# Expert attention units: the scores for the row maxima computed for two heads at once, in the two 64-row halves of TensorE's array

## The chip, the cores and the metric

The kernel runs on one core of one Trainium2 chip. The metric is device time in microseconds; the kernel before took 4004.94 us (median of 3 runs, 4000.94 to 4005.34). TensorE is PE in the profile, its weight loads PEld, VectorE DVE, ScalarE ACT, GpSimd POOL, and SyncE, which issues most DMAs, SP.

## What is computed

A two-layer model on x of 4 x 1024 tokens x 256 channels, all float32, each block behind a layer norm and added to x:

1. causal attention, 16 heads of 16, with a per-head linear position bias;
2. a mixture of four attention experts: a router picks the top 2 of 4 experts for each token, and each expert runs full (not causal) attention over the tokens of one batch that chose it:

```
q, k, v = xg @ wq[e] + bq[e], xg @ wk[e] + bk[e], xg @ wv[e] + bv[e]
att = softmax(where(valid_key, einsum(q, k) * 0.5, -1e9))
out += weight * (att @ v @ wo[e] + bo[e])      # scattered back to the tokens
```

3. causal attention with rotary positions;
4. a mixture of 64 small gated networks, top 8, capacity 128, beside a shared one.

## The kernel before, in words

The change touches block 2. Its 16 expert units (4 batches x 4 experts) run one after the other, sorted by size. A unit has `nt` tiles of 128 gathered tokens. There are three kinds of program: the first unit, the 14 middle ones, and the final one, each written out for every `nt` from 1 to 8; a run jumps from unit to unit through a barrier of all engines. In this run the 14 middle units have 7 tiles (4 units), 6 tiles (3), 3 tiles (4) and 2 tiles (3); the first unit has 6 tiles and the final one 2.

Within a unit, heads go in four groups `g` of four heads. Each group goes through two passes.

- **Pass 1** (task `s1`, L817 on PE) computes the scores with queries on partitions, only for the row maxima. q and k are float32 values split into three bfloat16 parts (hi, mid, lo) that lie under each other on the partitions of QS and KS, so that a matmul over 96 rows adds six part products; row 96 is the mask of the valid keys, and so a score matmul has 99 rows. A task fills one of two PSUM slots of two banks: one head with all its keys if there are over 512, two heads if over 256, four otherwise. One DVE reduction (L1086) per task takes the maxima into M. After a group's last one, `mh` and `ml` (L1094, L1099) split the negated maxima in two bfloat16 parts, `mt` (L827) transposes them, ACT copies them to MR, and a DMA that POOL issues (`mr`, L620) writes them into rows 99 and 100 of QS.
- **Pass 2** goes in key tiles `kt` and chunks of up to 512 queries `qc`; such a pair is called a round here. In a round, four `s2` matmuls (L835, 101 rows, one per head) write scores minus maximum into three single PSUM banks in turn, ACT takes the exponentials (L1023), and one `pv` task (L857, eight float32 matmul instructions of 17 columns, four heads in four column strips of the array) adds the products with the values. The result goes through `po` (ACT), `nt` (a PE transpose into one of pass 1's two slots, then DVE), and at the unit's end `yt` and `op` (L879, L1155).

Pass 1 of groups 1 to 3 runs in the unit itself, beside pass 2 of the groups before; pass 1 of group 0 of the *next* unit runs at the end, beside pass 2 of group 3. For that the next unit's rows are transposed (`xt`), projected (`qp`, L748), split on POOL (`spl`), stored to DRAM (`qs`, L1594, SP) and loaded back as the stacked rows of QS and KS (`ql`, L1610, SP, three DMAs for each of q and k and each group); `mk` (L1671) loads the mask rows. `nv` and `nr` on SP fetch the next weights and rows.

Each engine takes its tasks in one common order. That order is written by `unit_order`: every task gets a due time in a time scale of its own (`step` for one group of pass 2, `pace` for one group of pass 1, `turn` for the way from pass 1 to pass 2), and the list is sorted by it. PE, DVE, ACT and SP each work strictly down their part of the list, so a task that waits holds up all behind it on its engine.

## Time and profile before

| | |
|---|---|
| median of 3 runs | 4004.94 us |
| the profiled execution | 3994.29 us, its span 3992.6 us |
| mean granted TensorE clock | 0.932 of full speed |
| to about 840 us | block 1 |
| from there to 1018.6 us | the first unit |
| 1018.6 us to 2663.5 us | the 14 middle units |
| 2663.5 us to 2727.6 us | the final unit |
| from there to the end | blocks 3 and 4 |

The trace is one execution. A row of a timeline gives start, duration, engine, line, operation, output and inputs, the number of instructions that were merged into it, and in brackets how long the engine was idle before it and on whom it waited. A row of the windows gives the stretch, its length, the busy time of PE, PEld, DVE, ACT and POOL with their instructions, the granted clock, the DMA share and GB/s. The duration of a matmul holds the length of the pipeline, so what one costs in a stream is read from the distance of starts, not from its duration. The boundaries of the units are the ends of the last L1155 of each.

### The profile page before, as it was taken

The numbers are of one execution on the slowest core, as the hardware profiler recorded it, in microseconds if no ns is written. First come the engines' busy times: TensorE is split into PE (matmuls) and PEld (weight loads), VectorE is DVE, ScalarE is ACT, GpSimd is POOL, SyncE is SP. The second block draws the span as 40 slices with busy tenths as digits, with TensorE's granted clock in tenths as the row PEclk, the third lists the DMA queues.
The fourth block names the chain that finished last, engine by engine and source line by source line (L and its number), as shares of the span: only waits on it lengthen the run. The fifth ranks groups of instructions, "written<-read, shape, count | busy, mean of one in ns | idle before, by whom it ended". The sixth has DMA issues, their size and how long they took to land.

```text
span 3992.6 us, 56810 instructions
## 1 busy us (share of the span) xinstructions
PE 3415.7 (86%) x21573; PEld 1652.4 (41%) x21574; DVE 2375.3 (59%) x3496; ACT 2091.3 (52%) x4546; POOL 988.4 (25%) x845
## 2 busy tenths in 40 slices
PE   6999999878899999998899888764799888888895
PEld 3444445333434333334334334332344344445674
DVE  5565655656575757575675554333767878785323
ACT  2666665545576666665665554331465455551221
POOL 1241522322202020202111123232434141200574
PEclk8999999979999999999999999776899999998897
DMA  6454536323313030303313134334333232203588
GB/s 187 151 163 124 156 102 203 83 81 88 88 28 95 22 95 22 95 22 88 77 42 84 46 102 115 101 106 103 97 91 114 77 108 58 85 27 121 138 196 227
DMA packets 307098, 399.90 MB, mean 100 GB/s; under 512 B 33677, under 2 KB 271931, under 8 KB 299893
## 3 DMA queue, kind: packets, MB, share of 16 engines
q1 hardware_dynamic: 275718, 341.63, 30.9%
q0 software_dynamic: 26880, 50.49, 5.4%
q10 hardware_dynamic: 4224, 4.19, 0.3%
q8 instruction: 162, 2.65, 0.3%
q14 instruction: 114, 0.93, 0.1%
HBM read 230.48 MB, written 156.17 MB: 97 GB/s over the span
## 4 chain that ended last, share of the span: by engine, by line
PE 60%; DVE 19%; DMA 10%; issue 4%; ACT 3%; SPq 2%; POOL 2%; ACTq 0%; DVEq 0%; another core or an unknown queue 0%; POOLq 0%
PE PSUM L857 15%; PE PSUM L817 12%; DVE M L1086 11%; PE PSUM L835 11%; PE PSUM L748 6%; DMA KS<-mk_d 6%; PE PSUM L879 3%; PE PSUM L794 2%; PE PSUM L656 2%; DVE best L1455 1%; PE PSUM L865 1%; DVE XR L1458 1%; PE PSUM L820 1%; SPq L1610 1%; PE PSUM L838 1%
## 5 line engine op out<-in xcount | busy, mean ns | idle before, releaser
L1086 DVE TENSOR_REDUCE M<-PSUM 128x1 f32<-128x896 f32 (+7 forms) x1702 | 1703.3, 1032 | 994.1 <-PE PSUM L817 565.8
L1023 ACT ACTIVATE P<-PSUM 128x512 f32<-128x512 f32 (+2 forms) x3520 | 1582.2, 502 | 784.5 <-PE PSUM L835 521.0
L817 PE MATMUL PSUM<-KS,QS 99*128 99x512 bf16 (+3 forms) x3592 | 937.2, 343 | 253.1 <-DVE M L1086 89.0
L835 PE MATMUL PSUM<-QS,KS 101*128 101x512 bf16 (+2 forms) x3520 | 1067.7, 341 | 44.1 <-ACT P L1023 15.5
L857 PE MATMUL PSUM<-P,VA 128*17 128x384 f32 (+3 forms) x7040 | 769.0, 516 | 0.0
L835 PEld LDWEIGHTS PSUM<-QS,KS 101*128 101x128 bf16 x3520 | 331.5, 98 | 760.2 <-ACT P L1023 388.9
L817 PEld LDWEIGHTS PSUM<-KS,QS 99*128 99x128 bf16 x3592 | 316.9, 100 | 668.1 <-DVE M L1086 292.6
L748 PE MATMUL PSUM<-XT,W 128*128 128x512 f32 (+2 forms) x656 | 299.7, 585 | 13.0 <-DMA W<-in_L_ffn_wk 12.1
L708 POOL TENSOR_TENSOR QF<-QF,PH 128x1024 f32<-128x1024 f32 (+4 forms) x94 | 154.5, 1644 | 626.1 <-ACT PH L988 585.6
L620 POOL DMA_DIRECT2D QS<-MR x63 | 35.9, 569 | 933.8 <-ACT MR L1015 933.8
L857 PEld LDWEIGHTS PSUM<-P,VA 128*17 128x17 f32 x7040 | 135.0, 96 | 233.0 <-issue 202.3
L820 PE MATMUL PSUM<-identb,maskB 128*128 128x128 bf16 x1024 | 216.4, 226 | 0.0
L838 PE MATMUL PSUM<-maskB,identb 128*128 128x128 bf16 x1024 | 213.5, 224 | 0.0
L987 ACT ACTIVATE QF<-PSUM,bq 128x512 f32<-128x512 f32 (+2 forms) x132 | 82.1, 622 | 175.7 <-PE PSUM L748 175.5
L748 PEld LDWEIGHTS PSUM<-XT,W 128*128 128x128 f32 x656 | 124.4, 205 | 102.5 <-issue 75.8
L1002 ACT ACTIVATE VA<-PSUM 128x512 f32<-128x512 f32 (+1 forms) x72 | 41.3, 574 | 233.2 <-PE PSUM L794 233.2
L712 POOL TENSOR_TENSOR PH<-QF,PH 128x1024 bf16<-128x1024 f32 (+4 forms) x94 | 154.3, 1642 | 7.5
L794 PE MATMUL PSUM<-W,XT 128*128 128x256 f32 x544 | 142.4, 417 | 0.0
L879 PE MATMUL PSUM<-W,YT 128*128 128x256 f32 x544 | 134.8, 396 | 8.8 <-ACT YT L969 8.8
L656 PE MATMUL PSUM<-XT,KS 128*128 128x512 f32 x256 | 124.7, 637 | 14.2 <-DVE KS L1171 14.2
L1034 ACT ACTIVATE OT<-PSUM 128x512 f32<-128x512 f32 (+2 forms) x160 | 85.4, 534 | 89.4 <-PE PSUM L857 89.4
L820 PEld LDWEIGHTS PSUM<-identb,maskB 128*128 128x128 bf16 x1024 | 103.0, 101 | 68.8 <-issue 10.2
(213 smaller groups left out, 3085.7 us busy)
## 6 DMA issues: line engine op xcount, KB each, us to landing
qk_d<-PH SPq DMA_DIRECT2D x120, 256.0 KB
xg_d<-GX SPq DMA_DIRECT2D x19, 1152.0 KB, 12.8
yg_d<-GX SPq DMA_DIRECT2D x17, 1152.0 KB, 8.9
XF<-xg_d SPq DMA_DIRECT2D x17, 1024.0 KB, 7.0
VA<-n_L_ffn_expert_gate_up_w SPq DMA_DIRECT2D x64, 256.0 KB, 5.7
QS<-qk_d SPq DMA_DIRECT2D x36, 384.0 KB, 6.0
KS<-qk_d SPq DMA_DIRECT2D x36, 384.0 KB, 6.1
qk_d<-PH SPq DMA_DIRECT2D x48, 224.0 KB
```

The lines of the kernel that those rows point to most:

```text
L656: mm = e.matmul(s[:, x, :], WGU[:, k, IS * x + 128 * m:IS * x + 128 * m + 128], XT[:, k, 512 * c:512 * c + 512], start=(k == 0), stop=(k = ...
L708: e.tensor_tensor(f, f, hi, ALU.subtract).then_inc(S[name], 1)
L748: return e.matmul(out_, W[:, wi, k, cols:cols + 128], XT[:, k, a:a + n], start=(k == 0), stop=(k == 1))
L794: mm = e.matmul(s[:, 256 * x:256 * x + 256], XT[:, k, 128 * t:128 * t + 128], W[:, 2, k, :], start=(k == 0), stop=(k == 1))
L817: mm = e.matmul(slot_heads(s, hb)[:, x, a:b], QS[0:KA, g, h + x, 128 * qt:128 * qt + 128], KS[0:KA, g, h + x, a:b], start=True, stop=not d ...
L820: mm = e.matmul(slot_heads(s, hb)[:, x, kn - 128:kn], maskB[:, :], identb[:, :], start=False, stop=True, skip_group_check=True)
L835: mm = e.matmul(s[:, 0:q1 - q0], KS[0:KB, g, j, 128 * kt:128 * kt + 128], QS[0:KB, g, j, q0:q1], start=True, stop=not diag, skip_group_che ...
L838: mm = e.matmul(s[:, 0:128], identb[:, :], maskB[:, :], start=False, stop=True, skip_group_check=True)
L857: mm = e.matmul(PO[32 * j:32 * j + 17, a:b], VA[:, par, kt, 4 * g + j, :], P[:, n % NP, 0:q1 - q0], start=(kt == 0), stop=(kt == kts[-1]), ...
L879: mm = e.matmul(s[:, 256 * x:256 * x + 256], YT[:, k, 128 * t:128 * t + 128], W[:, 3, k, :], start=(k == 0), stop=(k == 1))
L1023: e.activation(P[:, m % NP, 0:q1 - q0], s[:, 0:q1 - q0], ACT.Exp, scale=ly.scale).then_inc(S["act_p"], 1)
L1086: e.tensor_reduce(m[:, qt, h:h + hb], v[:, :, 0:kn], AX.X, ALU.max).then_inc(S["dve_a"], 1)
```

## The change

Pass 1 of the middle units (`paired`) is computed otherwise.

- **The matmuls.** Two heads stand in the two 64-row halves: rows 0 to 48 and rows 64 to 112 of two new views, Q1 (in COS and SIN, which are free in block 2) and K1 (in the half of VA that units don't use). Each half holds three leading part products (q hi x k mid, q mid x k hi, q hi x k hi) and a mask row: 49 rows in place of 99. A task `s1` is now one chunk of up to 512 keys of a pair of heads: two matmuls, one for each half, into the two banks of a slot. With over four tiles a query tile has four such tasks (two pairs, two chunks), with three or four tiles two, with one or two tiles one task holds both pairs.
- **The reduction** takes both heads of a task in one instruction. With over four tiles there are two maxima per head, one for each chunk (M and the new MX); `mh` then first takes the larger of the two in one more DVE operation with a wait of its own.
- **The loads.** A new task `qa` on SP loads Q1 and K1, two buffers in turn (`g % 2`): four DMAs for each of q and k and each group, and for the next unit's two groups one more for the mask rows. `ql` and `mk` stay. The first unit loads the ones rows once (`on1`) and the pair rows of group 1.
- **The waits.** A paired `s1` waits for its `qa` and no longer for `ql` and `mk`. `qa` of a unit's group 3 waits for the last score of group 1, that of the next unit's groups 0 and 1 for the last scores of groups 2 and 3. `qs` also waits for the `qa` that read what it overwrites. In the final unit a memset (`vo`) sets back the ones in VA.
- **The order.** `step` for over four tiles is 0.76 nt² in middle units (0.84 before). `grouped` takes the sorted list of a middle unit with over four tiles and holds back each `s1`: two are let out ahead of the fourth `s2` of a round, two more ahead of a `pv` if over three are held, two ahead of another task that uses PSUM if over one is held, and all of them ahead of `mh`. Small middle units keep their order on PE. The final unit with up to four tiles has a time scale of its own again: `step` max(0.84 nt², 3.4), `pace` equal to it and `turn` 8.0, where it had 0.6 nt² + 2 nt, three quarters of it, and 5.5.

```diff
-    step = 0.6 * nt * nt + 2.0 * nt if small else 0.84 * nt * nt
-    pace, turn = (0.75 * step, 5.5) if small else (step, 8.0)
+    paired = not (layer.first or layer.final)
+    close = small and not layer.final
+    step = 0.6 * nt * nt + 2.0 * nt if close else max((0.76 if paired else 0.84) * nt * nt, 3.4)
+    pace, turn = (0.75 * step, 5.5) if close else (step, 8.0)
...
+    if paired:
+        ev += [(-1.2 + 0.1 * w, ("qa", 1, w, 2)) for w in range(2)]
+        ev += [(done[1] + 0.3 + 0.1 * w, ("qa", 1, w, 3)) for w in range(2)]
...
+                if paired:
+                    ev += [(max(done[2], back) + 0.1 + 0.1 * w, ("qa", 2, w, 0)) for w in range(2)]
+                ev += [(max(done[3], back, 52.0 * layer.first) + 0.5 + 0.1 * w, ("qa", 2, w, 1)) for w in range(2)]
...
+def grouped(tasks):
+    held, out = [], []
+    for task in tasks:
+        kind = task[0]
+        if kind == "s1":
+            held.append(task)
+            continue
+        if kind == "mh":
+            count = len(held)
+        elif kind == "s2":
+            count = 2 if task[-1] == 3 else 0
+        elif kind == "pv":
+            count = 2 if len(held) > 3 else 0
+        elif kind in PE_ACT or kind in PE_DVE:
+            count = 2 if len(held) > 1 else 0
+        else:
+            count = 0
+        out += held[:count]
+        held = held[count:]
+        out.append(task)
+    return out + held
...
+                elif kind == "s1" and O.paired:
+                    c, m = k // 2, ly.wide(k // 2)
+                    for x, duo in enumerate((0, 1) if ly.nt <= 2 else (k % 2,)):
+                        for half in range(2):
+                            r = slice(64 * half, 64 * half + 49)
+                            mm = e.matmul(s[:, half, m * x:m * x + m], Q1[g % 2][r, duo, 128 * qt:128 * qt + 128],
+                                          K1[r, g % 2, duo, 512 * c:512 * c + m], start=True, stop=True)
                     mm.then_inc(S["pe_a"], 1)
...
+                    if O.halves(i) == 2:
+                        e.tensor_tensor(M[:, g % 2, 0:ly.nt, :], M[:, g % 2, 0:ly.nt, :], MX[:, g % 2, 0:ly.nt, :],
+                                        ALU.max).then_inc(S["dve_x"], 1)
+                        e.wait_ge(S["dve_x"], O.at("dve_x", *task) - 1)
...
+                    for half in range(2):
+                        for r, m0, m1 in ((0, 0, 2), (32, 0, 1)) if wi == 0 else ((0, 1, 3), (32, 2, 3)):
+                            part = slice(64 * half + r, 64 * half + r + 16 * (m1 - m0))
+                            e.dma_start(Q1[b][part, :, 0:n] if wi == 0 else K1[part, b, :, 0:n],
+                                        qk_d[wi][m0:m1, :, 4 * g + half:4 * g + 4:2, 0:n].rearrange(
+                                            "m d h n -> (m d) h n")).then_inc(done, 16)
```

## Rows read from the trace of the kernel before

**Rows 1.** Page: busy time of the engines, and the chain that ended last.
```profile
PE 3415.7 (86%) x21573; PEld 1652.4 (41%) x21574; DVE 2375.3 (59%) x3496; ACT 2091.3 (52%) x4546; POOL 988.4 (25%) x845
...
PE 60%; DVE 19%; DMA 10%; issue 4%; ACT 3%; SPq 2%; POOL 2%; ACTq 0%; DVEq 0%; another core or an unknown queue 0%; POOLq 0%
```
**Rows 2.** Windows of 7-, 6-, 3-, 2-tile and final unit: engines' busy us, clock, DMA.
```profile
1415.50:1610.70 195.20, 181.61 (x1072) 70.00 (x1072) 125.94 (x142) 129.99 (x264) 25.93 (x23) 1.00 0.24 60
2124.00:2280.90 156.90, 144.06 (x924) 62.51 (x924) 95.81 (x125) 100.94 (x231) 23.54 (x23) 0.98 0.27 65
2402.30:2460.30 58.00, 47.63 (x272) 22.76 (x272) 27.99 (x45) 30.03 (x70) 16.40 (x23) 0.94 0.40 107
2566.10:2614.10 48.00, 35.13 (x188) 20.16 (x188) 14.28 (x27) 17.76 (x53) 14.01 (x23) 0.75 0.39 102
2663.50:2727.60 64.10, 38.60 (x185) 21.37 (x186) 25.05 (x65) 17.06 (x48) 21.11 (x23) 0.63 0.35 103
```
**Rows 3.** Groups of a 7-tile unit: count, busy, mean ns, idle before and releasers.
```profile
L1086 DVE TENSOR_REDUCE M<-PSUM 128x1 f32<-128x896 f32 x112 | 117.1, 1086 | 52.8 <-PE PSUM L817 52.5
L1023 ACT ACTIVATE P<-PSUM 128x512 f32<-128x512 f32 (+1 forms) x224 | 108.9, 544 | 36.6 <-PE PSUM L835 35.3
...
L817 PE MATMUL PSUM<-KS,QS 99*128 99x512 bf16 x224 | 61.1, 354 | 5.0 <-DVE M L1086 2.6 <-SPq L2034 1.7 <-DVE ON L1143 0.3
...
L835 PEld LDWEIGHTS PSUM<-QS,KS 101*128 101x128 bf16 x224 | 20.0, 96 | 55.0 <-ACT P L1023 32.0 <-issue 7.1 <-ACT PH L988 1.9
L817 PEld LDWEIGHTS PSUM<-KS,QS 99*128 99x128 bf16 x224 | 19.3, 98 | 35.4 <-DVE M L1086 15.8 <-issue 4.5 <-DVE ON L1143 2.0
```
**Rows 4.** Timeline of PE in that unit, in two stretches.
```profile
1529.74 0.54 PE L817 MATMUL PSUM<-KS,QS 99*128 99x512 bf16 x2
1530.13 0.38 PE L835 MATMUL PSUM<-QS,KS 101*128 101x512 bf16 x1
1530.35 0.54 PE L817 MATMUL PSUM<-KS,QS 99*128 99x512 bf16 x2
1530.72 0.38 PE L835 MATMUL PSUM<-QS,KS 101*128 101x512 bf16 x1
1531.03 0.62 PE L857 MATMUL PSUM<-P,VA 128*17 128x512 f32 x4
...
1531.47 0.61 PE L857 MATMUL PSUM<-P,VA 128*17 128x512 f32 x4
1532.02 0.39 PE L835 MATMUL PSUM<-QS,KS 101*128 101x512 bf16 x1
```
**Rows 5.** Timeline of DVE: pass 1 of the unit's group 3.
```profile
1516.87 2.09 DVE L1086 TENSOR_REDUCE M<-PSUM 128x1 f32<-128x896 f32 x2 [6.61 <-PE PSUM L817]
...
1523.26 3.09 DVE L1086 TENSOR_REDUCE M<-PSUM 128x1 f32<-128x896 f32 x3
1526.69 3.09 DVE L1086 TENSOR_REDUCE M<-PSUM 128x1 f32<-128x896 f32 x3 [0.34 <-PE PSUM L817]
1530.33 2.09 DVE L1086 TENSOR_REDUCE M<-PSUM 128x1 f32<-128x896 f32 x2 [0.55 <-PE PSUM L817]
...
1550.87 0.18 DVE L1094 TENSOR_SCALAR MHL<-M 128x28 bf16<-128x28 f32 x1
```
**Rows 6.** The reduction's group in a 6-tile and in a 2-tile unit.
```profile
L1086 DVE TENSOR_REDUCE M<-PSUM 128x1 f32<-128x768 f32 x96 | 87.6, 953 | 44.8 <-PE PSUM L817 44.6
...
L1086 DVE TENSOR_REDUCE M<-PSUM 128x4 f32<-128x1024 f32 x8 | 9.8, 1223 | 15.5 <-PE PSUM L817 15.5
```
**Rows 7.** SP in a 2-tile unit: one load run of its timeline, then its waits.
```profile
2571.28 2.82 SPq L1610 DMA_DIRECT2D KS<-qk_d  x6
...
SPq L1671 <- PE PSUM L835: 5.0, 1, 5.0
SPq L2031 <- DVEq L2026: 4.4, 1, 4.4
```
**Rows 8.** Timeline of PE in the final unit.
```profile
2693.14 0.37 PE L827 MATMUL PSUM<-identb,MHL 128*8 128x128 bf16 x2 [7.07 <-DVE MHL L1099]
```

More of the change, by code:

```diff
@@ L36 @@
             + [f"mrow{g}" for g in range(4)]
+            + ["pair_ones"] + [f"pair{w}{b}" for w in range(2) for b in range(2)]
             + ["sh_rows", "sh_weights", "first_weights"] + [f"sh_res{b}" for b in range(B)])
@@ L137, in __init__ @@
         self.front = 2 if layer.name == "moe" else 0
+        self.paired = layer.name == "moe" and not layer.first and not layer.final
     def ahead(self, i):
@@ L184, in raises, with halves, pair_loads, last_score @@
                 }[kind]
+    def halves(self, i):
+        return 2 if self.paired and self.layer.of(i).nch == 2 else 1
+    def pair_loads(self, i, wi, g):
+        return f"ahead_pair{wi}" if (i, g) == (2, 1) else f"pair{wi}{g % 2}"
+    def last_score(self, i, g):
+        ly = self.layer.of(i)
+        return "s1", i, g, ly.nt - 1, ly.duos()[-1] if self.paired else 4 - ly.heads(ly.nt - 1)
     def first_keys(self, ix):
@@ L287, in first_pass @@
     cost = [75 + 1.04 * layer.keys(qt) * layer.heads(qt) for qt, h in tiles]
+    if paired:
+        tiles = [(qt, k) for qt in range(layer.nt) for k in layer.duos()]
+        cost = [1.0] * len(tiles)
     done = 0
@@ L297, in first_pass, with attention_steps @@
     return ev
-def attention_steps(layer, i, first, second):
+def attention_steps(layer, i, first, second, paired=False):
     ev = []
@@ L305, in attention_steps @@
         if first[g]:
-            ev += first_pass(layer, i, g, *first[g])
+            ev += first_pass(layer, i, g, *first[g], paired)
         t0, long = second[g]
@@ L471, in unit_order @@
     over = [t + 1.06 * step for t, _ in second]
-    ev += attention_steps(layer, 1, first, second)
+    ev += attention_steps(layer, 1, first, second, paired)
+    done = [0.0] + [first[g][0] + 0.82 * first[g][1] for g in range(1, 4)]
+    if paired:
+        ev += [(-1.2 + 0.1 * w, ("qa", 1, w, 2)) for w in range(2)]
+        ev += [(done[1] + 0.3 + 0.1 * w, ("qa", 1, w, 3)) for w in range(2)]
+    if layer.first:
+        ev.append((50.0, ("on1", 2)))
+    if layer.final:
+        ev.append((0.02, ("vo", 1)))
     ev += [(-1.0 + 0.1 * w + 0.05 * g, ("ql", 1, w, 2 + g)) for w in range(2) for g in range(2)]
@@ L509, in unit_order @@
     ev.append((max(t for t, task in ev if task[0] == "op") - 0.1, ("kd", 1)))
+    tasks = [ev[k][1] for _, k in sorted((x[0], k) for k, x in enumerate(ev))]
     order = Order(layer)
-    for _, k in sorted((x[0], k) for k, x in enumerate(ev)):
-        order.add(*ev[k][1])
-    return order
+    for task in grouped(tasks) if paired and not small else tasks:
+        order.add(*task)
+    return order
+def grouped(tasks):
[19 more added lines that the diff above has]
+    return out + held
 def build(nc, d, out):
@@ L1583, in attention_sp @@
                     w.wait_ge(*O.split(i, wi, g2))
+                    if O.paired and g2 == 0:
+                        w.carried(f"ahead_pair{wi}", 64 + 16 * wi)
+                    elif O.paired:
+                        for g in (2, 3):
+                            w.wait_ge(f"pair{wi}{g % 2}", "qa", 1, wi, g)
                     for g in (2 * g2, 2 * g2 + 1):
```

73 lines of the change are left out of this document (68 added, 5 removed), and 2 rows, old and new, of the table ONE_BANK.

## The prediction

> **What bounds the kernel now.** I read the busy shares and the chain first. PE is busy for 86% of the span and holds 60% of the chain, DVE holds 19% [rows 1]. So PE is the first suspect, but the units differ, and the change lies in 14 of them alone. The windows come next, one unit each [rows 2]. A 7-tile unit takes 195.2 us with PE at 182, ACT at 130, DVE at 126, at full clock. A 6-tile unit takes 156.9 us and looks the same. A 3-tile unit takes 58.0 us with PE at 48, a 2-tile unit 48.0 us with PE at 35 and the clock at 0.75: there no engine is full, and the unit is a chain of waits. Units of 7 and 6 tiles hold 4 x 195.2 + 3 x 156.9 = 1251 us, and that is where pass 1 is worth something.
>
> The groups of a 7-tile unit say how full PE really is [rows 3]. Before a pass 1 weight load PE's queue waited 15.8 us for DVE, before a pass 2 load 32.0 us for ACT. The view of the starts [rows 4] gives costs in a stream: an s2 matmul of 512 queries holds the array 0.22 us (1530.13 to 1530.35), a pass 1 task of 896 keys 0.37 us (1530.35 to 1530.72).
>
> Last, DVE in pass 1 of group 3, where the projections are out of the way [rows 5]. From 1516.87 to 1550.87, 34.0 us, it does the 28 reductions of a group at 1.086 us each [rows 3], 30.4 us, and two evacuations of nt of some 0.65 us: 93% of the stretch. The distances say it too: a run of three reductions lasts 3.43 us (1523.26 to 1526.69), of which 3.26 us is DVE's own. A run of two takes 2.50 us (1530.33 to 1532.83), and DVE is idle for 0.3 to 0.55 us between runs. So where pass 1 runs densely, DVE is the bound already and PE a close second; PE alone binds where only two tasks fall into a round, and ACT where there are none.
>
> **Pass 1 on PE.** Halving the stream: 224 matmuls of a 7-tile unit become 112 concurrent pairs, so 112 x 0.37 = 41.4 us become 20.7 us, if the two halves run at once. The trace has no row tiling. It has four column strips at once: the four halves of a pv begin together (one row of x4, the next four only 0.44 us later, [rows 4]), and that is the nearest row. The bounds are all of the 20.7 us and nothing of it; I take all.
>
> But the array has to be set over for it. The pv shows the price: it starts 0.31 us after an s2 that streams 0.22 us, so 0.09 us going in; from its second x4 at 1531.47 to the next s2 at 1532.02 are 0.55 us where 0.44 us streams, so 0.11 us coming out [rows 4]. That is 0.20 us for each excursion. The Trainium skill ("TensorEngine Tiling (Array Packing)", Key Properties) says that changing the tiling mode drains TensorE while changing the tile doesn't; the pv rows agree. By that page alone, without a price, one would put the saving at the full 20.7 us.
>
> Bounds of the price in the new place: 0 (a burst that stands beside a pv may share its drain) and 0.20 us; I take 0.20. With two tasks in a row a burst costs 0.37 + 0.20 = 0.57 us against 0.74 us: 0.17 us saved, x 56 bursts = 9.5 us per 7-tile unit. For 6 tiles a task has 768 keys, 0.37 x 768/896 = 0.32 us: 0.32 + 0.20 against 0.64, 0.12 us x 48 = 5.8 us. With 3 tiles the order isn't grouped: a task of 0.32 us becomes 0.16 + 0.20, 0.04 us dearer, x 24 = +1.0 us. With 2 tiles 0.42 us becomes 0.21 + 0.20: nothing. PE's demand falls by 4 x 9.5 + 3 x 5.8 - 4 x 1.0 = 51 us. With no drain at all it would be about 83 + 47 + 15 + 5 = 150 us, and with no concurrency it rises by (56 x 4 + 48 x 3 + 24 x 4 + 8 x 3) x 0.20 = 98 us.
>
> **What DVE lets through.** DVE reduces the same elements with the same number of instructions: per query tile two tasks of 1024 and two of 768 elements (7 tiles), 2 x 1.22 + 2 x 0.95 = 4.35 us [rows 6], against 4 x 1.086 = 4.34 us. The extra maximum in mh is one small operation, about 0.18 us as its neighbour L1094 [rows 5], with its wait 0.2 us x 4 x 7 units = 5.6 us of DVE; it stands on the way from the last reduction to mt, where the rounds without pass 1 (the 6.61 us DVE gap, [rows 5]) cover it. Without that cover it costs its 5.6 us.
>
> DVE can give only the 7% of the dense stretch in which it is idle, 2.3 us of 34. And bursts feed it less evenly. A reduction starts 0.59 us after a task of two matmuls in a row (1529.74 to 1530.33, [rows 4, 5]), 0.37 us after a pair. Two tasks fill both slots, and the next burst's second task needs the second slot back: 0.37 + 2 x 1.22 = 2.8 us later. A round with one burst on PE is 4 x 0.22 + 0.99 + 0.09 + 0.57 = 2.53 us (the 0.99 is the pv to the next s2), against 0.88 + 0.99 + 0.09 + 0.74 = 2.70 us now: so it saves some 0.15 us. Where three tasks fell in a round before, the grouped order now has rounds of two and some of four. In those of four the third and fourth wait for both slots and PE stands, at 1.1 us per task as before. So I let half of PE's saving through in 7-tile units, -5 us each, -20 in all. In 6-tile units, where the burst saves less and its 1024-element reductions are the same 1.22 us, I take -1 each, -3. The same skill page (PSUM Bottleneck) warns that tiling speeds up TensorE but not the evacuation of PSUM, and here that is this paragraph.
>
> **The new loads.** 32 DMAs and two mask loads more per middle unit, on SP. SP issues six in 2.82 us [rows 7], 0.47 us each: 34 x 0.47 = 16 us on top of about 26 us in a 2-tile unit of 48.0. They take SP's slack: qa of group 2 stands ahead of all ql at the unit's start (3.8 us), qa of group 3 ahead of the first qs, and the next unit's four qa around mk and ql. Behind them queue qs, whose stores feed the next loads. SP now waits 5.0 us for PE at mk and 4.4 us for DVE at the unit's end [rows 7], and each 3.8 us of new issue falls ahead of one of these. So I cost the loads at nothing, and up to +3 us in each of seven small units (+21) if the slack is misjudged; in large units SP has over 100 us idle. Against it paired s1 no longer waits for ql and mk, up to -1.3 us in a 2-tile unit. With the +1.0 us of 3-tile drains: 0 for all small units. The first unit gets 11 DMAs, +1.
>
> **The final unit** (64.1 us, clock 0.63 [rows 2]) issues the same work in another order. PE stood 7.07 us for DVE's mh [rows 8], which was queued behind sums (x2) that wait for gathers. With the shorter scale the second and third mh come two or more x2 earlier, while transposes and projections of the next layer go behind attention. Bounds: -7 and, if these are late, +5; I take -2.
>
> **Sum.** -20 - 3 + 0 + 1 - 2 = -24 us on 3994.3 us of the profiled execution (span 3992.6), that is 3970. The median of the runs lies 10.6 us above that execution, so -24 gives 3981 for the median.
>
> **Rivals.**
> - *All of PE's saving arrives, or more.* Units of 7 tiles are PE-bound in the projection stretches, and the reduction starts 0.2 us sooner. Then -38 - 17 - 2 = -57: 3948, and with shared drains down to 3925. For it: PE 93% busy, 60% of the chain. Against it: DVE at 93% in the dense stretch.
> - *DVE stands idle between bursts and paces the units (slower).* Place: rounds of pass 1 with over four tiles. Both slots fill at once and then PE is away at s2 and pv; DVE's idle time is now 0.15 us per reduction (0.34 to 0.55 us in runs of two or three), and would be at least 0.37 / 2 plus the rest of the round, some 0.25 us. It decides if more than two thirds of the tasks lie in DVE-bound rounds. Price 0.1 us x (4 x 112 + 3 x 96) = 74 us, less a fifth where PE paces: +45 to +60, 4055. The same sign and less has SP's late loads, +20.
> - *The halves don't run at once.* +98 us of PE's demand, about two thirds of it on the path: 4070. Against it only the column strips speak.
> - *No net change.* The PE saving goes into new waits for slots, the small units' drains and loads: 4005 +/- 8.
>
> **Chances.** The forecast with partial gain (3950 to 3995) 0.45; all the gain (below 3950) 0.17; no change 0.16; slower by DVE's idling or SP 0.18; no concurrency 0.04. A difference under 0.2% (8 us) can't be told from none. Faster 0.62, same 0.16, slower 0.22. The range 3930 to 4035 leaves out the top of the slow cases and the lowest gains. The forecast's own range is 3950 to 3995.
>
> **What would show it.** Right: in the middle units two L817-like matmuls start within 0.01 us of each other; a burst of four matmuls takes 0.55 to 0.6 us from the s2 before it to the s2 behind it; DVE's total is unchanged; 7-tile units last 188 to 192 us, 6-tile units 154 to 157, 3-tile units 57 to 60, 2-tile units 46 to 50; the final unit about 62. Wrong: 7-tile units under 185 us would mean that DVE was not the second bound, and over 197 us that the bursts starve it; small units over 3 us longer with PE waiting for L817's loads would put it on SP.

## The result, and the profile after

The changed kernel takes 4121.09 us (median of 3 runs, 4119.03 to 4126.41) against 4004.94 us before: 1.0296 times as long, 95% interval 1.0272 to 1.0319. It is 116 us slower, where 24 us faster was forecast. The profiled execution took 4121.09 us (span 4119.4), 127 us over the one of before.

The page after, to be held against [rows 1]: the busy lines, the granted TensorE clock in tenths in 40 slices of the span, and the chain by engine. The last line is the clock of the page before.

```profile
PE 3448.4 (84%) x21573; PEld 1570.9 (38%) x21574; DVE 2377.8 (58%) x3525; ACT 2087.4 (51%) x4546; POOL 988.0 (24%) x845
...
PEclk8999999989989999999999998977699999999897
...
PE 57%; DVE 19%; DMA 11%; issue 4%; SPq 3%; ACT 3%; POOL 2%; ACTq 0%; another core or an unknown queue 0%; DVEq 0%; POOLq 0%
```
```profile
PEclk8999999979999999999999999776899999998897
```

DVE's work is the same (2377.8 against 2375.3 us). PE is busy for 33 us more although it streams less. Windows of one unit each, columns as in [rows 2]: two 7-tile units, a 6-, a 3-, a 2-tile unit and the final one.

```profile
1472.01:1689.42 217.41, 189.99 (x1072) 60.70 (x1072) 125.90 (x146) 129.05 (x264) 25.88 (x23) 0.92 0.27 66
1689.42:1901.10 211.68, 184.41 (x1072) 59.93 (x1072) 125.89 (x146) 128.86 (x264) 25.89 (x23) 0.94 0.29 68
...
2069.84:2233.90 164.06, 144.04 (x924) 53.19 (x924) 96.22 (x129) 100.54 (x231) 23.51 (x23) 0.95 0.30 76
...
2465.20:2526.00 60.80, 50.60 (x272) 21.67 (x272) 27.60 (x44) 30.13 (x70) 16.41 (x23) 0.89 0.46 122
...
2696.50:2746.50 50.00, 34.08 (x188) 17.59 (x188) 14.33 (x28) 17.72 (x53) 14.01 (x23) 0.76 0.44 113
...
2795.10:2851.40 56.30, 29.67 (x163) 16.52 (x164) 25.51 (x66) 13.27 (x42) 20.87 (x23) 0.70 0.39 117
```

| units | before, us | after, us | difference |
|---|---|---|---|
| 7 tiles, four | 201.5, 195.3, 195.2, 195.3 | 220.3, 214.7, 217.4, 211.6 | +77 |
| 6 tiles, three | 160.9, 157.1, 156.9 | 168.8, 164.1, 164.0 | +22 |
| 3 tiles, four | 62.9, 58.5, 57.9, 57.7 | 67.3, 60.8, 60.6, 59.4 | +11 |
| 2 tiles, three | 48.1, 48.0, 49.4 | 50.6, 50.0, 48.6 | +4 |
| final | 64.1 | 56.2 | -8 |

These differences add up to 106 us. The first unit ended 18 us later too. That can't be put down to the change: over the executions profiled below its end lies anywhere from 1018 to 1037 us, both in kernels built from the one before (1019 to 1033 us) and in those built from the changed one (1018 to 1037 us). What remains is mostly in the large units, those of 7 and 6 tiles. There the granted clock was 1.00 and 0.98 in [rows 2] and is now 0.91 to 0.94 in the 7-tile units and 0.94 to 0.95 in the 6-tile ones.

The timeline of PE in a dense stretch of the first of these two 7-tile units, then DVE's of the same stretch (start, duration, instructions; in brackets the idle time before and its releaser).

```profile
1542.50 0.34 PE L872 MATMUL PSUM<-VA,COS 49*128 49x384 bf16 x2 [0.80 <-DVE M L1171]
1542.77 1.56 PE L812 MATMUL PSUM<-XT,W 128*128 128x384 f32 x4
1544.26 1.05 PE L935 MATMUL PSUM<-P,VA 128*17 128x512 f32 x8
1545.24 0.61 PE L913 MATMUL PSUM<-QS,KS 101*128 101x512 bf16 x2
1545.78 0.39 PE L872 MATMUL PSUM<-VA,COS 49*128 49x512 bf16 x2
1546.10 0.61 PE L913 MATMUL PSUM<-QS,KS 101*128 101x512 bf16 x2
...
1548.17 0.55 PE L872 MATMUL PSUM<-VA,COS 49*128 49x512 bf16 x4
1548.66 0.61 PE L913 MATMUL PSUM<-QS,KS 101*128 101x512 bf16 x2
1549.88 0.34 PE L872 MATMUL PSUM<-VA,COS 49*128 49x384 bf16 x2 [0.62 <-DVE M L1171]
1550.75 0.39 PE L872 MATMUL PSUM<-VA,COS 49*128 49x512 bf16 x2 [0.53 <-DVE MX L1171]
```
```profile
1542.36 1.81 DVE L1171 TENSOR_REDUCE MX<-PSUM 128x2 f32<-128x768 f32 x2
1546.21 1.23 DVE L1171 TENSOR_REDUCE M<-PSUM 128x2 f32<-128x1024 f32 x1 [2.04 <-PE PSUM L872]
1548.60 1.22 DVE L1171 TENSOR_REDUCE M<-PSUM 128x2 f32<-128x1024 f32 x1 [1.16 <-PE PSUM L872]
1549.75 1.81 DVE L1171 TENSOR_REDUCE MX<-PSUM 128x2 f32<-128x768 f32 x2
```

Three things are in these rows. The halves do run at once: a pair of two 512-key matmuls holds PE for 0.32 us (1545.78 to 1546.10), a burst of four for 0.49 us (1548.17 to 1548.66). The burst is two matmuls of 512 keys and then two of 384 (the reductions behind it are of 1024 and 768 elements); a pass 1 task of one head before, 512 and 384 keys one after the other, took 0.37 us [rows 4], so the four in a row would take 0.74 us. PE and DVE stand idle in turn: DVE idles 2.04 us while PE does projections and pv, then the burst comes, and PE idles 0.62 and 0.53 us for DVE. And behind a burst other tasks that use one of the two slots wait as well, as the groups of this unit show (to be held against [rows 3]; busy us and mean ns, then the idle time before and its releasers):

```profile
L1171 DVE TENSOR_REDUCE M<-PSUM 128x2 f32<-128x1024 f32 x56 | 67.2, 1220 | 55.3 <-PE PSUM L872 55.3
L1171 DVE TENSOR_REDUCE MX<-PSUM 128x2 f32<-128x768 f32 x56 | 52.0, 951 | 15.1 <-PE PSUM L872 14.9
...
L872 PE MATMUL PSUM<-VA,SIN 49*128 49x512 bf16 (+1 forms) x112 | 18.2, 377 | 5.4 <-DVE M L1171 3.3 <-DVE MX L1171 1.6 <-DVE ON L1244 0.5
L872 PE MATMUL PSUM<-VA,COS 49*128 49x512 bf16 (+1 forms) x112 | 17.5, 357 | 4.6 <-DVE M L1171 3.5 <-DVE MX L1171 0.8
...
L943 PE MATMUL PSUM<-ident,OT 128*128 128x128 f32 x28 | 5.1, 303 | 4.6 <-DVE M L1171 2.2 <-DVE MX L1171 1.7 <-ACT OT L1115 0.6
L905 PE MATMUL PSUM<-identb,MHL 128*8 128x128 bf16 x28 | 2.2, 218 | 4.5 <-DVE MHL L1196 4.5
```

PE stood idle ahead of nt (L943) for 0.7 us in a unit without the regrouping (e1 below) and for 4.6 us here; ahead of mt (L905), which needs a group's last reduction, for 2.0 and 4.5 us.

For each kernel below I split the third 7-tile unit by the distances from each PE start to the next. "Stream" is what the columns take at 2.4 GHz, "clock" the extra where the granted clock was 1.2 GHz, "gaps" the rest; of the gaps, those at a passage from pass 2 to pass 1 (s2 to s1) and back have a column of their own. All times are in us.

| kernel | stream | clock | gaps | of them s2 to s1, s1 to s2 | us at half clock | unit |
|---|---|---|---|---|---|---|
| before | 158.3 | 0 | 36.9 | 7.2, 0.8 | 0 | 195.2 |
| after | 137.4 | 15.9 | 64.1 | 9.4, 5.1 | 34 | 217.4 |
| e1 planner's order | 137.4 | 1.9 | 56.0 | 13.7, 9.9 | 3 | 195.3 |
| e11 two, not later | 137.4 | 4.3 | 59.3 | 7.6, 5.3 | 10 | 201.0 |
| e10 held, singly | 137.4 | 7.9 | 63.0 | 9.9, 6.0 | 20 | 208.3 |
| e3 before, regrouped | 158.3 | 3.4 | 47.0 | 3.4, under 0.8 | 7 | 208.7 |
| e6 pairs twice | 158.3 | 4.9 | 58.6 | 8.7, 4.6 | 10 | 221.8 |
| e4 after, half reduced | 137.4 | 0 | 52.2 | 6.3, 5.2 | 0 | 189.7 |
| e8 e1, half reduced | 137.4 | 1.7 | 48.3 | 10.4, 9.9 | 3 | 187.5 |
| e5 before, half reduced | 158.3 | 0 | 29.1 | 1.7, 0.7 | 0 | 187.4 |
| e14 before, 35 rows | 158.3 | 1.7 | 48.8 | 11.2, 8.1 | 3 | 208.8 |

One unit is a small sample where the clock is concerned. Over all seven large units the traces give, in us:

| kernel | four 7-tile units | of them at half clock | three 6-tile units | of them at half clock |
|---|---|---|---|---|
| before | 787 | 7 | 475 | 17 |
| after | 864 | 126 | 497 | 55 |
| e1 planner's order | 782 | 10 | 466 | 7 |
| e11 two, not later | 814 | 58 | 505 | 68 |
| e10 held, singly | 837 | 85 | 529 | 116 |
| e3 before, regrouped | 847 | 51 | 512 | 61 |
| e6 pairs twice | 894 | 51 | 538 | 68 |
| e4 after, half reduced | 765 | 7 | 463 | 27 |
| e8 e1, half reduced | 752 | 14 | 456 | 20 |
| e13 loads, no pair | 787 | 7 | 469 | 7 |

### The profile page after: what moved, and what is told of

It reads as the page before. It is cut to its first block, busy times and chain, and to the rows that moved or that the text cites. A ratio compares the mean times of both kernels' runs of the same rounds, so it can differ in the third digit from the quotient of the medians.

```text
span 4119.4 us, 57404 instructions
## 1 busy us (share of the span) xinstructions
PE 3448.4 (84%) x21573; PEld 1570.9 (38%) x21574; DVE 2377.8 (58%) x3525; ACT 2087.4 (51%) x4546; POOL 988.0 (24%) x845
## 4 chain that ended last, share of the span: by engine, by line
PE 57%; DVE 19%; DMA 11%; issue 4%; SPq 3%; ACT 3%; POOL 2%; ACTq 0%; another core or an unknown queue 0%; DVEq 0%; POOLq 0%
PE PSUM L935 14%; PE PSUM L913 12%; DMA KS<-mk_d 8%; DVE M L1179 7%; PE PSUM L895 5%; PE PSUM L812 5%; DVE M L1171 4%; PE PSUM L872 4%; PE PSUM L858 3%; PE PSUM L957 2%; DVE MX L1171 2%; PE PSUM L720 2%; ACT P L1104 1%; DVE best L1556 1%; SPq L1716 1%
## 5 line engine op out<-in xcount | busy, mean ns | idle before, releaser
L1179 DVE TENSOR_REDUCE M<-PSUM 128x1 f32<-128x768 f32 (+7 forms) x846 | 854.4, 1034 | 529.0 <-PE PSUM L898 416.0
L935 PE MATMUL PSUM<-P,VA 128*17 128x384 f32 (+3 forms) x7040 | 796.3, 532 | 0.0
L1171 DVE TENSOR_REDUCE M<-PSUM 128x2 f32<-128x1024 f32 (+1 forms) x464 | 530.6, 1165 | 415.6 <-PE PSUM L872 414.6
L913 PEld LDWEIGHTS PSUM<-QS,KS 101*128 101x128 bf16 x3520 | 313.4, 99 | 912.3 <-ACT P L1104 499.7
L895 PE MATMUL PSUM<-KS,QS 99*128 99x512 bf16 (+3 forms) x1832 | 487.2, 346 | 183.2 <-DVE M L1179 65.4
L1171 DVE TENSOR_REDUCE MX<-PSUM 128x2 f32<-128x768 f32 (+1 forms) x368 | 303.3, 847 | 109.4 <-PE PSUM L872 108.0
L895 PEld LDWEIGHTS PSUM<-KS,QS 99*128 99x128 bf16 x1832 | 165.9, 102 | 358.7 <-issue 145.4
L898 PE MATMUL PSUM<-identb,maskB 128*128 128x128 bf16 x1024 | 217.4, 227 | 0.0
L872 PE MATMUL PSUM<-VA,SIN 49*128 49x512 bf16 (+2 forms) x880 | 135.9, 354 | 74.6 <-DVE M L1171 26.7
L872 PE MATMUL PSUM<-VA,COS 49*128 49x512 bf16 (+2 forms) x880 | 135.2, 352 | 23.3 <-DVE M L1171 17.3
```

The source lines that it names most:

```text
L872: mm = e.matmul(s[:, half, m * x:m * x + m], Q1[g % 2][r, duo, 128 * qt:128 * qt + 128], K1[r, g % 2, duo, 512 * c:512 * c + m], start=Tru ...
L895: mm = e.matmul(slot_heads(s, hb)[:, x, a:b], QS[0:KA, g, h + x, 128 * qt:128 * qt + 128], KS[0:KA, g, h + x, a:b], start=True, stop=not d ...
L898: mm = e.matmul(slot_heads(s, hb)[:, x, kn - 128:kn], maskB[:, :], identb[:, :], start=False, stop=True, skip_group_check=True)
L913: mm = e.matmul(s[:, 0:q1 - q0], KS[0:KB, g, j, 128 * kt:128 * kt + 128], QS[0:KB, g, j, q0:q1], start=True, stop=not diag, skip_group_che ...
L935: mm = e.matmul(PO[32 * j:32 * j + 17, a:b], VA[:, par, kt, 4 * g + j, :], P[:, n % NP, 0:q1 - q0], start=(kt == 0), stop=(kt == kts[-1]), ...
L1171: e.tensor_reduce(top[:, 2 * (k % 2):2 * (k % 2) + 2], s[:, :, 0:m], AX.X, ALU.max).then_inc(S["dve_a"], 1)
```

## Experiments

**e1: pairs without regrouping**, against VectorE's half work (e4) and twice the stream (e6).

```diff
-    for task in grouped(tasks) if paired and not small else tasks:
+    for task in tasks:
```

> The changed kernel, but the units over four tiles take their tasks in the planner's own order: pass-1 pairs are no longer moved together in twos. Theory A (the bursts of two hold the score slots, VectorE can't empty them in time, and TensorE waits at its next tile): the four 7-tile units come back from 212 to 220 us to 195 to 200, the three 6-tile units from 164 to 169 to about 158, and the kernel from 4121 to about 4030 to 4045. Theory B (the granted clock falls in these units because TensorE streams less, whatever the order): the 7-tile units stay at 210 us or more, each still with some 25 to 37 us at half clock, and the kernel stays at 4105 us or more, since 9 us of drains a unit are added again. Mixed case, half of each: about 4080.

Measured: 4011.57 us (10 runs), ratio to before 1.0009 (0.999 to 1.0029). The same units as above:

```profile
1427.95:1623.27 195.32, 181.06 (x1072) 61.40 (x1072) 126.45 (x146) 128.86 (x264) 25.94 (x23) 0.99 0.30 74
1975.96:2129.39 153.43, 141.38 (x924) 52.94 (x924) 96.88 (x129) 101.49 (x231) 23.56 (x23) 1.00 0.32 82
2350.06:2411.04 60.98, 50.66 (x272) 21.69 (x272) 27.59 (x45) 30.13 (x70) 16.46 (x23) 0.89 0.48 121
```

The regrouping is the loss: 4121 to 4012 us, below what theory A had said, and the clock is back although PE streams as little as in the change. So a shorter stream alone doesn't lower it here. But the pairs alone bring nothing either.

**e4: half of the reduction.** The changed kernel, reading half of each score tile (the units of two tiles are edited in the same way).

```diff
-                        e.tensor_reduce(top[:, 2 * (k % 2):2 * (k % 2) + 2], s[:, :, 0:m],
+                        e.tensor_reduce(top[:, 2 * (k % 2):2 * (k % 2) + 2], s[:, :, 0:m // 2],
```

> The changed kernel, but every pass-1 reduction of the middle units reads only the first half of each head's keys (the row maxima are then those of half of the keys); the order, the pairs and TensorE's work are the same. A reduction over 1024 elements a partition takes 1.22 us now and should take some 0.65 us, so a 7-tile unit has about 30 us less of VectorE work. Theory A (VectorE empties the slots too slowly after a burst): the 7-tile units fall from 212 to 220 us to 190 to 198, slot waits behind a pass-1 pair go from 9 us to under 3 a unit, kernel about 4020 to 4040. Theory B (clock, following TensorE's shorter stream): time at half clock in these units stays at 25 to 37 us each, the 7-tile units stay over 207 us, kernel over 4085.

Measured: 3981.28 us, ratio 0.9948 (0.9931 to 0.9965). The 1.22 us reductions take 0.69 us, the 7-tile unit 189.7 us at clock 1.00, the gaps between s1 and s1 fall from 8.7 to 4.0 us (theory A had under 3, and a slower kernel). With slots coming back sooner the same order takes 28 us less a unit, and the time at half clock goes with the stalls, from 181 to 34 us in the large units. Not all of the 28 us is the bursts': half reductions alone, with nothing regrouped, give 8 us (e8 below against e1). Held against e8, the regrouping costs 19 us in the seven large units where it costs 113 with whole reductions. So theory A holds: it is slots that come back too slowly that make the regrouping dear, and the clock falls behind these stalls.

**e6: each pair twice.**

```diff
-                    for x, duo in enumerate((0, 1) if ly.nt <= 2 else (k % 2,)):
+                    for x, duo in enumerate((0, 1) if ly.nt <= 2 else (k % 2,) * (2 if ly.nt > 4 else 1)):
+                        x = x if ly.nt <= 2 else 0
```

> The changed kernel, but in units over four tiles each concurrent pair of pass 1 is issued twice in a row with the same result, so that TensorE streams as long in pass 1 as it did before the change (41 us a 7-tile unit in place of 21), in the changed order. Theory A (slots and VectorE): the slots are held 0.2 us longer each time, TensorE gets about 20 us more to do in a unit in which it already waits; the 7-tile units grow by 5 to 20 us each, kernel 4150 to 4210. Theory B (the clock falls because TensorE streams less between its stalls): the 7-tile units go back to under 10 us at half clock each, their length stays within 5 us of the changed kernel's 212 to 220 or falls, kernel 4090 to 4135.

Measured: 4193.2 us, ratio 1.0475 (1.0457 to 1.0493); 7-tile units 222 to 229 us. Theory A's time came true. In this 7-tile unit the longer stream had 10 us at half clock in place of 34, so the clock's extra went from 15.9 to 4.9 us; but the 20.9 us of stream stood on the path. The 6-tile units don't bear out theory B: they had 68 us at half clock with the longer stream and 55 with the shorter one.

**e2: the final unit's scale alone**, on the kernel before.

```diff
-    step = 0.6 * nt * nt + 2.0 * nt if small else 0.84 * nt * nt
-    pace, turn = (0.75 * step, 5.5) if small else (step, 8.0)
+    close = small and not layer.final
+    step = 0.6 * nt * nt + 2.0 * nt if close else max(0.84 * nt * nt, 3.4)
+    pace, turn = (0.75 * step, 5.5) if close else (step, 8.0)
```

> The kernel before with one part of the change alone: the final unit's time scale. Theory A (the final unit's gain of 7.9 us in the changed kernel is its own order's): final unit 56 to 58 us in place of 64.1, all other units as before, kernel about 3997 (ratio 0.998). Theory B (the gain came from the other edits to that unit: loads that were already there, a clock that stood otherwise when it began): final unit 62 to 65 us, kernel within 0.1% of before.

Measured: 4004.91 us (12 runs), ratio 1.0008 (0.9997 to 1.0019). Half a hit: the final unit takes 57.6 us in place of 64.1, but the kernel isn't faster. The profiles show where it goes. Before, all 16 of the next layer's transposes (L769) and 11 of its first 16 projection matmuls (L748) start inside the final unit; in e2 it is 5 of the transposes and none of the projections, and the last projection matmul (L794) starts 15.2 us behind the unit's end in place of 9.2. So 6.0 of the 6.5 us are given back at once. From the start of the final unit to the end of the span four kernels with the old scale take 1320 to 1329 us (mean 1325), eleven with the new one 1324 to 1334 us (mean 1329).

**e3: regrouping alone**, on the kernel before with its unpaired tasks (`grouped` is added as in the change).

```diff
-    for _, k in sorted((x[0], k) for k, x in enumerate(ev)):
-        order.add(*ev[k][1])
+    tasks = [ev[k][1] for _, k in sorted((x[0], k) for k, x in enumerate(ev))]
+    for task in grouped(tasks) if not (layer.first or layer.final or small) else tasks:
+        order.add(*task)
```

> The kernel before, with only the regrouping added: in the middle units over four tiles its own (unpaired) pass-1 tasks, one head each, are put two in a row where the changed kernel puts its pairs. TensorE streams in pass 1 as long as before (41.8 us a 7-tile unit). Theory A (two pass-1 tiles in a row take both two-bank slots, and everything that needs one waits for VectorE; the clock falls after these stalls): 7-tile units 205 to 220 us in place of 195.3, with over 10 us at half clock each, kernel 4060 to 4130. Theory B (it takes the short half-array pairs to do harm, because TensorE then has too little to stream; grouping alone saves the passages between s1 and s2): 7-tile units 190 to 197 us at full clock, kernel 3985 to 4010.

Measured: 4095.62 us, ratio 1.0228 (1.021 to 1.0245).

```profile
1460.49:1669.22 208.73, 185.06 (x1072) 70.62 (x1072) 125.68 (x143) 129.79 (x264) 25.95 (x23) 0.98 0.22 56
...
2051.34:2218.67 167.33, 147.86 (x924) 62.19 (x924) 95.37 (x125) 101.63 (x231) 23.57 (x23) 0.96 0.25 61
```

Theory A: it needs no pair to do the harm. With the full stream this 7-tile unit had 7 us at half clock (theory A had said over 10; the four have 7 to 21), the changed kernel's 34. In the 6-tile units the full stream had 61 us and the halved one 55.

**e10: the same rule, one at a time.**

```diff
-            count = 2 if task[-1] == 3 else 0
+            count = 1 if task[-1] == 3 else 0
...
-            count = 2 if len(held) > 3 else 0
+            count = 1 if len(held) > 2 else 0
...
-            count = 2 if len(held) > 1 else 0
+            count = 1 if len(held) > 0 else 0
```

> The changed kernel with the same regrouping rule, but one pair at a time where it let two go: pairs still wait for the last head of an s2 group, never two in a row. Theory A (the size of the burst against two slots does the harm): 7-tile units 193 to 198 us with under 7 us at half clock, kernel 4000 to 4020, as without any regrouping (4012). Rival (their place right behind the four s2 heads does it, where ScalarE is busy and the slots come free late): 7-tile units 205 us or more, kernel over 4060.

Measured: 4125.32 us, ratio 1.0298 (1.0281 to 1.0315). Theory A failed as I had put it, and the rival's figures were met. But the kernel was a poor test of either. One release for each s2 group is too few (a unit has 112 tasks and 56 groups); the held ones are let go together before mh. PE's timeline at a group's end:

```profile
1502.65 0.34 PE L872 MATMUL PSUM<-VA,SIN 49*128 49x384 bf16 x2 [1.11 <-DVE M L1171]
1503.78 0.34 PE L872 MATMUL PSUM<-VA,SIN 49*128 49x384 bf16 x2 [0.79 <-DVE M L1171]
...
1506.26 0.90 PE L905 MATMUL PSUM<-identb,MHL 128*8 128x128 bf16 x7 [1.87 <-DVE MHL L1196]
```

Three or four tasks then run at DVE's speed, one each 1.13 us (1502.65 to 1503.78), and mt comes 1.87 us late. So lateness looks like a cost of its own beside the burst's size. Whether the place behind the four s2 matters too, as the rival had it, wasn't tried. The next kernel leaves the lateness out.

**e11: two in a row, none later than planned.** The second task of each two is pulled forward; the old rule's lines are left out here.

```diff
+        out.append(task)
+        if task[0] == "s1":
+            for other in tasks[x + 1:]:
+                if other[:3] == task[:3] and other not in ahead:
+                    out.append(other)
+                    ahead.add(other)
+                    break
```

> The changed kernel with another rule of regrouping in all middle units: each second pass-1 task of a head pair is pulled forward to stand right behind the first, so that two come in a row as in the change, but none is later than the planner put it (the change holds them back to the end of an s2 group, at most two there, so pass 1 can fall behind and mt with it). Theory A (two two-bank tiles in a row against two slots do the harm, wherever they stand): 7-tile units 205 us or more, kernel over 4070. Theory B (the holding back does it: the last reduction of a head, and with it mh, mt and the next head's s2, come late): 7-tile units 186 to 196 us, since about half of the 182 passages at 0.11 to 0.15 us are saved; kernel 3975 to 4020.

Measured: 4056.84 us, ratio 1.0154 (1.0127 to 1.0181); third 7-tile unit 201.0 us, a 6-tile unit 166.4. It lies between the theories. The idle time ahead of mt is now 1.0 us a unit, but s1 after s1 costs 11.8 us in 56 bursts, 0.21 us each, which is all that a saved excursion is worth. In the kernel's time half of the regrouping's loss is there with two in a row alone (1.0009 to 1.0154), and the other half comes with the holding back (1.0154 to 1.0296). The units say that it isn't so clean a cut. The 7-tile units grow by 31 us with two in a row and by 50 more with the holding back, the 6-tile units by 39 and then shrink by 8. And the direct wait is paid for by the passages saved: over the seven large units s1 after s1 costs 77 us more than in e1 and the passages 75 us less. The 70 us by which these units are longer than in e1 are then some 46 of clock and 20 of other waits.

**e8 and e5: what bounds the units when nothing is regrouped.** e8 is e1, e5 the kernel before, both with reductions over half of the keys.

```diff
+                    kn = kn // 2 if moe and i != 2 * O.final and not O.layer.first and not O.layer.final else kn
                     e.tensor_reduce(m[:, qt, h:h + hb], v[:, :, 0:kn], AX.X, ALU.max).then_inc(S["dve_a"], 1)
```

The edit shown is e5's; e8's are those of e1 and e4.

> The changed kernel in the planner's own order (no regrouping), and the pass-1 reductions of the middle units read only half of each head's keys (the row maxima are then those of half of the keys). It tells what bounds the ungrouped units, which stayed at 193.6 us although TensorE streams 20.9 us less. Theory A (TensorE itself: 94 passages s2 to s1 at 0.145 us and 88 back at 0.113 us have replaced the stream): the 7-tile units stay at 190 to 194 us, kernel 3990 to 4010. Theory B (VectorE's reductions pace the slots): 7-tile units 178 to 187 us, kernel 3930 to 3975.

> The kernel before; the pass-1 reductions of the middle units read only the first half of each head's keys (the row maxima are then those of half of the keys): 1.09 us each become some 0.62, about 50 us less of VectorE work in a 7-tile unit. It tells whether VectorE paces the units before. Theory A (TensorE bounds them): 7-tile units 193 to 195.3 us, kernel 3990 to 4006. Theory B (VectorE's reductions pace the slots): 7-tile units 189 us or less, kernel under 3975.

Measured: e8 3961.3 us, ratio 0.9886 (0.9868 to 0.9905); e5 3922.73 us, ratio 0.9821 (0.98 to 0.9841). A 7-tile unit of e8, then of e5:

```profile
1413.53:1601.01 187.48, 179.67 (x1072) 61.32 (x1072) 78.06 (x146) 128.47 (x264) 25.93 (x23) 0.99 0.31 77
```
```profile
1404.17:1591.54 187.37, 178.79 (x1072) 70.89 (x1072) 78.40 (x143) 129.37 (x264) 25.91 (x23) 1.00 0.26 62
```

Theory B came out in e5 (187.4 us, its kernel below B's bound) and all but came out in e8 (187.5 us where B had 178 to 187, the kernel's time where B had it). But DVE doesn't bound them alone: 48 us less of its work gave 8 of 195 us a unit. With DVE out of the way both units last the same, with 20.9 us less stream in one: the passages eat nearly all of the pairs' gain. In e5 an excursion costs 1.7/98 + 0.7/85 = 0.03 us of gaps, in e8 10.4/94 + 9.9/88 = 0.11 + 0.11 us. In e8 94 passages in and 88 out make 20.3 us, 17.9 more than in e5; of the other 3.0 us 1.7 are clock.

**e14: the passage without a pair.** The kernel before, pass 1 over its last 35 rows only.

```diff
-                            mm = e.matmul(slot_heads(s, hb)[:, x, a:b], QS[0:KA, g, h + x, 128 * qt:128 * qt + 128],
+                            ra = slice(64 if moe and not (O.layer.first or O.layer.final) else 0, KA)
+                            mm = e.matmul(slot_heads(s, hb)[:, x, a:b], QS[ra, g, h + x, 128 * qt:128 * qt + 128],
```

> The kernel before; in the middle units the pass-1 matmuls contract only over the last 35 of their 99 rows, which lie in the upper 64-row half of the array (the small part products but one are left out of the scores of which the row maxima are taken). Their number, width and order and VectorE's work are unchanged. Theory A (passing between a matmul on a 64-row half and one on the full array costs 0.11 us each way, pair or not): s2 to s1 and s1 to s2 become 0.10 to 0.15 us each, some 98 and 85 passages a 7-tile unit add 17 to 19 us in part hidden under VectorE's 7 us of waits: 7-tile units 207 to 214 us in place of 195.3, kernel 4070 to 4120. Theory B (the passages belong to the pairs, or to their two tiles): 7-tile units 194 to 197 us, kernel within 0.3% of before.

Measured: 4197.21 us, ratio 1.0493 (1.0441 to 1.0546); 7-tile units 207 to 214 us. The starts in one of them:

```profile
1552.75 0.61 PE L836 MATMUL PSUM<-QS,KS 101*128 101x512 bf16 x2
1553.29 0.55 PE L818 MATMUL PSUM<-KS,QS 35*128 35x512 bf16 x2
1553.77 0.39 PE L836 MATMUL PSUM<-QS,KS 101*128 101x512 bf16 x1
1554.09 0.55 PE L818 MATMUL PSUM<-KS,QS 35*128 35x512 bf16 x2
```

One s2 and the passage take 0.32 us (1553.77 to 1554.09) where [rows 4] has 0.22, the s1 task 0.48 where it has 0.37. Over the unit a passage costs 11.2/98 = 0.11 us in and 8.1/85 = 0.10 us out. So theory A holds for the 7-tile units: 0.11 us each way belongs to the change of the rows used (35 in one half, then 101), not to having two at once. The kernel's time lies above the 4120 us that theory A had at most, because the 6-tile units were beyond what I expected: they are told of below.

**e9 and e12: pairs in the large units alone, planner's order**; e12 also with the step 0.84.

```diff
+    def pairs(self, i):
+        return self.paired and self.layer.of(i).nt > 4
...
-    paired = not (layer.first or layer.final)
+    middle = not (layer.first or layer.final)
+    paired, soon = middle and nt > 4, coming.nt > 4 and not layer.final and coming.name == "moe"
...
-                elif kind == "s1" and O.paired:
+                elif kind == "s1" and O.pairs(i):
```

> Half-array pairs only in the middle units over four tiles, in the planner's own order; the middle units of two and three tiles compute pass 1 as before the change, without the added loads. Theory A (in the small units the pairs and their loads cost 1.4 to 4.3 us each, seven units 15 us together): the 3-tile units return to 57.7 to 59 us (first one 63), kernel 3990 to 4002, ratio to before 0.996 to 0.999. Rival (these differences move with the granted clock from execution to execution and aren't the pairs'): kernel 4006 to 4014, ratio 1.000 to 1.002.

> Pairs only in the middle units over four tiles, in the planner's own order (the kernel at 3994.5 us), with the step of these units as before the change, 0.84 in place of 0.76 times the square of the tiles. Theory A (TensorE and the passages set the pace and the order only has to be dense enough): same within 0.2%, 3987 to 4002 us. Theory B (the shorter step matters, because pass 1 has to run ahead): 7-tile units 2 us or more longer, kernel 4004 to 4015.

Measured: e9 3994.54 us (9 runs), ratio 0.9969 (0.9955 to 0.9982); e12 3985.61 us (12 runs) with before at 3994.31 us in the same job, ratio 0.9983 (0.9972 to 0.9994). By these ratios e9 is 12 us faster than the kernel before, and by the medians 127 us faster than the changed one. The step makes no difference that these runs can tell. Against e1 the small units give back what they had lost: 3 tiles 63.3, 58.2, 58.0, 57.8 us, for 67.2, 61.0, 60.7, 59.1.

**e13: all the loads, no pair.** Built on e9, with pairs nowhere and the loads everywhere.

```diff
     def pairs(self, i):
-        return self.paired and self.layer.of(i).nt > 4
+        return False
...
+                    for wi in range(2) if O.paired else ():
+                        if (i, g) == (1, 1):
+                            w.carried(f"ahead_pair{wi}", 64 + 16 * wi)
+                        else:
+                            w.wait_ge(f"pair{wi}{g % 2}", "qa", i, wi, g)
```

> Pass 1 in every unit as before the change, one head at a time in the planner's order with the step 0.84, but all the loads of the change stay (34 DMAs a middle unit into the rows for pairs, and TensorE waits for them before a head's pass 1, though it reads nothing of them). Theory A (SyncE and the queues have room for them, as the prediction had it): within 0.2% of before, small units as before (3 tiles 57.7 to 59 us, first of them 63). Theory B (they delay the other loads of the short units, or pass 1 waits for them): the 3-tile units 59 to 62 us and the 2-tile ones 50 us or more, kernel slower than before by 0.25 to 0.5%, 10 to 20 us.

Measured: 4029.02 us, ratio 1.0104 (1.0079 to 1.0129). A 7-tile unit takes 195.35 us, as before; the 3-tile units 72.5, 64.4, 62.6, 63.6. Theory B, and dearer than it said. SP's queue in a 3-tile unit of e13 (start, duration, issues), then the like one of before:

```profile
2352.21 0.42 SPq L800 DMA_DIRECT2D yg_d<-XR  x1
2353.40 1.75 SPq L1755 DMA_DIRECT2D COS<-qk_d  x4
2355.20 1.84 SPq L1755 DMA_DIRECT2D VA<-qk_d  x4
2357.08 2.81 SPq L1727 DMA_DIRECT2D QS<-qk_d  x6
2359.93 2.82 SPq L1727 DMA_DIRECT2D KS<-qk_d  x6
2362.96 0.82 SPq L1822 DMA_DIRECT2D KS<-mk_d  x1
2364.10 0.41 SPq L1866 DMA_DIRECT2D W<-in_L_ffn_wv  x1
```
```profile
2344.66 0.43 SPq L730 DMA_DIRECT2D yg_d<-XR  x1
2345.86 2.75 SPq L1610 DMA_DIRECT2D QS<-qk_d  x6
2348.66 2.81 SPq L1610 DMA_DIRECT2D KS<-qk_d  x6
2351.69 1.00 SPq L1671 DMA_DIRECT2D KS<-mk_d  x1
2353.02 0.41 SPq L1715 DMA_DIRECT2D W<-in_L_ffn_wv  x1
```

From the row's first issue to that of wv are 8.4 us before and 11.9 us with the loads: eight new issues stand ahead of ql, the mask and the weights and push them by some 3.6 us, and the unit grows by 5.9 us. Where the other 2.3 us arise wasn't traced. e13 also waits for more than the changed kernel does (ql and the pair's loads both), so its price is an upper one.

## Why the prediction was wrong, by its own steps

- *The halves run at once, 20.7 us of stream for a 7-tile unit.* Right: 158.3 to 137.4 us.
- *0.20 us for each excursion.* Right in size: 0.11 + 0.11 us (e8, e14). The Trainium skill ("TensorEngine Tiling (Array Packing)", Key Properties) has it that a change of the tiling mode drains TensorE. The 0.11 us at a passage in e14 agree with that. What I drew from it was the burst of two, which saves one excursion. On TensorE alone that is so: e11 saved 6 us at s2 to s1 and 5 us at s1 to s2, 0.19 us a burst.
- *"What DVE lets through": half of PE's saving, -5 us a 7-tile unit.* **This is the step that failed**, in sign. I had the rule in the text (two tasks fill both slots, the next must wait) and put it at nothing for rounds of two. e11 measures it at 0.21 us a burst, as much as the excursion saved; then holding tasks back to the end of an s2 group made mh and mt late, and nt waited for the same slots, which the step had no term for. Against e1 the regrouping costs 20 us a 7-tile unit and 10 us a 6-tile unit, 113 us in all; the runs say 1.0296 - 1.0009 = 0.0287, 115 us.
- *The clock had no term at all*, and it is the larger part of that loss. Of the 22 us between the third 7-tile units of e1 and after, 14 are clock: 15.9 against 1.9 us. Over the seven large units, split in the same way, some 65 of the 113 us are clock and 45 gaps; 3 can't be assigned. I took 1.00 in [rows 2] as given.
- *DVE is the bound already where pass 1 is dense.* Half right: halving its work gives 8 us of 195 (e5), not more.
- *Loads cost nothing, small units 0.* Wrong there, right in the large ones (195.35 us in e13). The bound of +21 was in the text; the seven small units cost 15 us more than before in e1 and 30 us more in e13.
- *Final unit -2, first unit +1.* The unit gained 6 to 8 us and the layer behind it gave them back (e2); the first unit's +1 can't be told apart in 19 us of spread.
- *The rivals.* "DVE stands idle between bursts" was the right one by kind and place, at +45 to +60 us with a chance of 0.18 shared with SP. Its price is near what e11 measured (+58 over e1), but that is luck: it was worked out from DVE's idle time alone, and in e11's large units most of the loss is clock. My own test, "over 197 us that the bursts starve it", pointed to it: the units were at 212 to 220.

The account, from e1 to the sum: in e1 the 7-tile units are 5 us shorter together, the 6-tile ones 9, the small ones 15 longer, final and what follows about 4 longer, together +5, against a measured ratio of 1.0009 (+4 us); then +113 by the regrouping. Of the 9 us the pairs' part is not shown: e13, without a pair, has 6 of them, with 7 us at half clock where the kernel before had 17.

How the clock falls is open in part. Without the regrouping, or with it and half reductions, the large units had 14 to 34 us at half clock in all, whatever they streamed (e14 is the exception, see the last section); with two in a row or held back and whole reductions they had 113 to 201. In the 7-tile units the shorter stream had more of it under the same rule (126 us after, against 51 in e3 and in e6), in the 6-tile units it had not (55 against 61 and 68). So what the shorter stream adds isn't settled, and no kernel varied the two finely enough to tell.

## What to carry to other kernels

Before you pack an array to save stream, count how often its rows change between neighbours: at 0.11 us each way against a task of 0.37 us, halving the task gives nothing. Before you group to save these passages, count the slots that the group takes at once and what else waits in the same ring; a task held back is also late for whatever ends its phase. Read the granted clock of the stretch after such a change of order: here it cost some 65 us where the waits cost 45. And an idle queue over a whole kernel says nothing about the first microseconds of a short stage.

## What the runs showed that was not expected

In e14's 6-tile units, where pass 1 uses 35 rows and is of 512 and 256 keys, the granted clock stayed at 0.50 for 51 and for 44 us on end, with PE busy for 98% of the time and for 95% of the 46 us before the first of them. The unit took 207 us in place of 157. The other two 6-tile units had 109 and 106 us at half clock, 99 us of it on end in the last one. The 7-tile units of the same kernel, with 512 and 384 keys, stayed at 0.98 to 1.00. Windows of a 7-tile unit, of the 46 us before the first long fall, and of that fall (the clock stands behind POOL's busy time):

```profile
1440.75:1649.52 208.77, 198.91 (x1072) 62.56 (x1072) 126.36 (x142) 132.82 (x264) 25.88 (x23) 0.99 0.23 56
...
2120.00:2166.00 46.00, 43.64 (x261) 14.00 (x261) 29.95 (x40) 29.50 (x66) 8.79 (x7) 1.00 0.22 56
2166.90:2218.10 51.20, 50.17 (x192) 9.65 (x191) 23.22 (x28) 19.70 (x45) 0.56 (x1) 0.50 0.07 15
```

So a PE that the profile shows as busy was granted 1.2 GHz here, and in the 46 us before this fall it had stood idle for 1.25 us at the longest. Why these units and not the longer ones wasn't tried.
